# Half of x1 on each expert row: a Mamba and mixture-of-experts kernel without its stored x1 rows

## The reference, cut to what matters

```
x1  = layernorm(x + attn(x))                 # 4096 rows of 256
w, e = softmax(top2(x1 @ gate_w + gate_b))   # two experts a row
ffn = w[0] * expert(e[0], x1) + w[1] * expert(e[1], x1)   # each with its bias b2
out = layernorm(x1 + ffn)
```

## Time and profile before

| | us |
|---|---|
| median of three runs | 1420.89 |
| span of the profiled execution | 1418.7 |
| PE busy | 1272.5 |
| DVE busy | 1090.1 |
| ACT busy | 804.2 |
| POOL busy | 791.7 |

### The profile page before, as it was taken

The page is one execution under the profiler, slowest core; times in us unless marked ns, Lnnn a source line. Parts: engine busy times, 40 slices in busy tenths (PEclk is TensorE's granted clock), DMA queues, the critical chain, the costliest instruction groups (busy, mean ns, idle before and its releaser), DMA issues.

```text
span 1418.7 us, 40444 instructions
## 1 busy us (share of the span) xinstructions
PE 1272.5 (90%) x13336; PEld 1050.7 (74%) x13337; DVE 1090.1 (77%) x2560; ACT 804.2 (57%) x1861; POOL 791.7 (56%) x751
## 2 busy tenths in 40 slices
PE   4889999999999999999888799999999999999970
PEld 2456666666667666666678799999999999999960
DVE  4889999999999999899967877565566656565536
ACT  4667666666666776667545344444454544444436
POOL 3467666767675877788774615234072406152772
PEclk9899999999999999999968999999999999999996
DMA  6213432333443233322235231303012312202594
GB/s 211 81 31 120 135 109 93 96 119 119 135 135 120 84 113 117 123 88 81 87 146 189 72 121 34 121 27 122 30 54 94 105 51 76 72 30 63 134 210 162
DMA packets 90547, 145.73 MB, mean 103 GB/s; under 512 B 9376, under 2 KB 73376, under 8 KB 90336
## 3 DMA queue, kind: packets, MB, share of 16 engines
q1 hardware_dynamic: 75104, 97.03, 21.4%
q0 software_dynamic: 15072, 46.51, 11.2%
q10 hardware_dynamic: 288, 1.19, 0.2%
HBM read 103.03 MB, written 41.67 MB: 102 GB/s over the span
## 4 chain that ended last, share of the span: by engine, by line
PE 48%; DVE 25%; issue 12%; POOL 6%; ACT 5%; DMA 1%; DVEq 1%; SPq 0%; ACTq 0%; POOLq 0%
PE pe L1101 12%; PE pa L1101 12%; PE py L1126 11%; DVE arena L1691 5%; DVE arena L1730 4%; POOL arena L2631 3%; PE pa L676 2%; DVE arena L1738 2%; PE pm L853 2%; PE py L815 2%; DVE arena L1757 2%; DVE arena L1744 1%; PE pt L835 1%; DVE arena L1664 1%; DVE arena L1645 1%
## 5 line engine op out<-in xcount | busy, mean ns | idle before, releaser
L1101 PE MATMUL pe<-arena 128*128 128x128 f16 x3408 | 219.4, 220 | 26.0 <-issue 26.0
L1101 PEld LDWEIGHTS pe<-arena 128*128 128x128 f16 x3408 | 203.4, 98 | 31.3 <-issue 30.6
L1101 PE MATMUL pa<-arena 128*128 128x128 f16 x3408 | 218.8, 220 | 0.0
L1553 ACT ACTIVATE arena<-pe,arena 128x128 f32<-128x128 f32 x568 | 162.0, 371 | 79.8 <-PE pe L1101 78.9
L1101 PEld LDWEIGHTS pa<-arena 128*128 128x128 f16 x3408 | 201.5, 98 | 0.0
L1126 PE MATMUL py<-arena 128*128 (+1 forms) x1704 | 197.7, 273 | 1.3 <-DVE arena L2337 0.9
L1691 DVE SCALAR_TENSOR_TENSOR arena<-pa,arena 128x511 f32<-128x511 f32 (+2 forms) x240 | 178.9, 746 | 11.6 <-ACT arena L1199 5.5
L1126 PEld LDWEIGHTS py<-arena 128*128 128x128 f16 x1704 | 163.4, 98 | 19.6 <-issue 1.8
L2300 DVE SCALAR_TENSOR_TENSOR pm<-pa,arena 128x128 f32<-128x128 f32 x284 | 80.5, 352 | 98.7 <-ACT arena L1553 88.0
L1730 DVE TENSOR_TENSOR_SCAN arena<-arena,pe 128x512 f32<-128x512 f32 x128 | 148.8, 1204 | 3.2 <-issue 1.8
L2531 POOL TENSOR_SCALAR arena<-arena 128x1536 f16<-128x1536 f32 (+2 forms) x35 | 42.6, 1218 | 189.3 <-DVE arena L2337 184.1
(11 more groups left out here) (309 smaller groups left out, 2539.5 us busy)
## 6 DMA issues: line engine op xcount, KB each, us to landing
arena<-step_rows SPq DMA_DIRECT2D x64, 512.0 KB, 6.3
arena<-in_w_exp POOLq DMA_DIRECT2D x32, 768.0 KB, 4.8
arena<-queue SPq DMA_DIRECT2D x74, 129.5 KB, 2.1
answer<-arena SPq DMA_DIRECT2D x71, 128.0 KB, 1.7
arena<-in_x SPq DMA_DIRECT2D x16, 512.0 KB, 6.2
answer<-zeros SPq DMA_DIRECT2D x10, 512.0 KB, 4.8
arena<-h SPq DMA_DIRECT2D x9, 512.0 KB, 5.5
h<-arena SPq DMA_DIRECT2D x8, 512.0 KB, 3.0
```

The lines of the kernel that those rows point to most:

```text
L1101: ins = pe.matmul(bank[:, f * P:(f + 1) * P], w_split[:, p, hl, d * 2 * FF + col:d * 2 * FF + col + P], x[:, r, d, :], start=(n == 0), sto ...
L1553: ins = e.activation(sg[:, half, f, :], GATE[half][:, f * P:(f + 1) * P], ACT.Silu, bias=b1a[:, bass.ds(ex_, 1), ff], scale=1.0 / S1)
```

## The change

The table `x1_rows`, its eight stores and the eight adding transfers are gone. Each token is in two expert rows, and each of the two now gets half of x1: ACT writes `x_half` = 0.5 times the x1 part of `xq` (`rows_halved`, in the place where it made `b_row`, one tile ahead), and DVE makes `b_row` = bias times weight plus `x_half` in a new `rows_added`. SP waits for `x_halved` too before it overwrites `xq`. `x_half` has three buffers of its own. DVE's wait for `x1_back` becomes one for `low_got`.

```
-                if u > NB:
-                    b = u - 1 - NB
-                    sp.wait_ge(x1_ready, b + 1)
-                    sp.dma_start(x1_rows[b * T:(b + 1) * T, :].rearrange("(k p) d -> p k d", p=P),
-                                 x1b[:, 1 - q, :, 0:D]).then_inc(stored[1 - q], 16)
...
             def swap_rows(i, r):
 
                 sp.wait_ge(w_ready, WB * i + (r + 1))
+                sp.wait_ge(x_halved, WB * i + (r + 1))
...
             def epilogue(st):
...
                 h_out(st, 1)
+                rows_halved(0, 0)
                 root_x1(st)
...
+            def rows_halved(i, r):
+
+                at_least(e, b_ready, WB * i + (r - 2))
+                e.activation(x_half[:, r % WB], xq[:, r % WB, 0:D], ACT.Copy, scale=0.5).then_inc(x_halved, 1)
...
                 high_part(i, r, 1)
-                e.wait_ge(w_ready, WB * i + (r + 1))
-                e.sem_inc(hop, 1)
-                e.activation(b_row[:, r], b2a[:, bass.ds(ex_, 1), :].rearrange("p o d -> p (o d)"), ACT.Copy,
-                             scale=w_row[:, r:r + 1]).then_inc(b_ready, 1)
+                rows_halved(i, r + 1)
...
+            def rows_added(i, r, ex_):
+
+                dve.wait_ge(x_halved, WB * i + (r + 1))
+                dve.wait_ge(w_ready, WB * i + (r + 1))
+                if isinstance(i, int) and i == 0 and r == 0:
+                    dve.wait_ge(bias_ready, 2)
+                dve.sem_inc(hop, 1)
+                dve.scalar_tensor_tensor(b_row[:, r], b2a[:, bass.ds(ex_, 1), :].rearrange("p o d -> p (o d)"),
+                                         w_row[:, r:r + 1], x_half[:, r], ALU.mult, ALU.add).then_inc(b_ready, 1)
+
             def second_half(i, r, ex_):
                 gated(i, r, 1, ex_)
+                rows_added(i, r, ex_)
                 low_part(i, r, 1)
...
                 if b == 0:
-                    dve.wait_ge(x1_back, 16 * NB)
+                    dve.wait_ge(low_got, 16 * NTILE)
...
-                if b == 0:
-                    pool.wait_ge(low_got, 16 * NTILE)
-                    for n in range(NB):
-                        pool.dma_start(total[:, n * NK:(n + 1) * NK], x1_rows[n * T:(n + 1) * T, :].rearrange(
-                            "(k p) d -> p k d", p=P), accum_op=ALU.add).then_inc(x1_back, 16)
```

More of the change, by code:

```diff
@@ L169, in build @@
     hx = nc.dram_tensor("hx", [NB, T, D], F32, kind="Internal").ap()
-    x1_rows = nc.dram_tensor("x1_rows", [NTOK, D], F32, kind="Internal").ap()
     queue = nc.dram_tensor("queue", [DUMMY + 4 * P, QW], F32, kind="Internal").ap()
@@ L305, in build @@
         xq = carve(WB, QW)
+        x_half = carve(WB, D)
         b2a = carve(NE, D)
@@ L432, in build @@
         need_ready = sem("need_ready")
-        x1_back = sem("x1_back")
         got = [sem(f"got{b}") for b in range(NB)]
@@ L436, in build @@
         w_half, w_ready, b_ready = sem("w_half"), sem("w_ready"), sem("b_ready")
+        x_halved = sem("x_halved")
         f_scale = sem("f_scale")
@@ L599, in _ @@
                 sp.wait_ge(w_ready, r + 1)
+                sp.wait_ge(x_halved, r + 1)
                 lead_rows(first, WB + r)
@@ L605, in _ @@
             for s in range(2):
-                sp.wait_ge(stored[s], 16 * NB + 16)
+                sp.wait_ge(stored[s], 16 * (NB // 2) + 16)
             with sp.Fori(1, NGRP) as i:
@@ L1257, in chunk_d @@
                 if c.k == 0:
-                    e.wait_ge(stored[c.q], 16 * c.st.h + 16)
+                    e.wait_ge(stored[c.q], 16 * (NB // 2 if c.layer == 1 else c.st.h) + 16)
                 e.wait_ge(out_full, c.n + 1)
@@ L1295, in x1_apply @@
                 before = st.h - 1 if wq == 1 else st.h
-                e.wait_ge(stored[wq], 16 * before + 16)
                 e.wait_ge(scattered[wq], 128 * (before - 4) + 16)
@@ L1583, in _ @@
             high_part(0, 0, 1)
-            e.wait_ge(w_ready, 1)
-            e.activation(b_row[:, 0], b2a[:, bass.ds(first, 1), :].rearrange("p o d -> p (o d)"), ACT.Copy,
-                         scale=w_row[:, 0:1]).then_inc(b_ready, 1)
+            rows_halved(0, 1)
             tile(0, 1, first)
```

## The result

The changed kernel takes 1413.34 us, the median of five runs (1410.45 to 1415.42). The kernel before took 1420.89 us beside it (1419.6 to 1422.71). The ratio is 0.9947, with a 95% interval from 0.9933 to 0.996: faster by 7.5 us, where 8.6 were forecast. The profiled run took 1414.7 us with a span of 1412.7, so 2.0 us lie around the span.

A forecast was written before the change was run, and what follows sets the result against it. PE bounds the expert loop, DVE has slack, and adding transfers crowd out PE's needs behind it. Terms -10.6 + 0.8 + 1.2 = -8.6 us take the median from 1420.89 to 1412.3 us, range 1408.3 to 1417.6.

The forecast's parts named there:

- The adding transfers: Behind the expert loop: without them PE's extra waits and the half clock go, gaining 10.6 us, bounds 4.3 and 12.3.
- 1.0 us that I left in place: PE behind the loop: one ordinary wait of 0.64 us and 0.4 us for new code were expected to stay.
- upper bound of 12.3 us: Tail gain if only the ordinary wait stays and each restart of PE saves its 0.2 us as well.
- the first rival: Behind the loop: the second gathers beside new code suffice for the longest gap; only 4.3 us gained, 1418.6 us; chance 0.11.
- DVE's waits for POOL: In POOL's seven bursts, 21 of the new DVE instructions, both inputs in SBUF, wait 1.0 us each on average.
- the bound of 3.1: The most that one new DVE instruction would wait for POOL in a burst: 3.1 us.
- What the waits cost PE in the loop: In the six bursts of the loop, DVE's late instructions cost 0.8 us, bounds 0 and 7.
- the slack: The queue-row load behind the store of `answer`: lands in 2.1 us, leaving 3.0 us before its `turn`.
- the slower rival: In the bursts DVE falls behind beyond the load's slack; its cost of up to 31 us lands on PE; chance 0.08.
- The early tiles: First burst, tiles 5 and 6: DVE runs late and the `turn` near 831 us waits longer; 1.2 us, bounds 0 and 3.
- ACT, SP and the Mamba stage: ACT's halving replaces an equal copy, and the eight stores and SP's 116.4 us of waiting go without effect: zero.
- The sum: Whole kernel: -10.6 + 0.8 + 1.2 = -8.6 us, span from 1418.7 to 1410.1 us.

The follow-up runs named there:

- experiments 1, 2 and 6: The runs no_adds, both_ways and plain_copy, in that order.
- no_adds: The kernel before without the eight adding transfers, x1 rows still stored, no new DVE instruction: 1410.4 us, ratio 0.9918.
- psum_half: The changed kernel with the new DVE instruction before the first `gated` and the halved x1 in PSUM instead of SBUF: 1410.5 us, ratio 0.9928.
- after_third: The changed kernel run a third time, unchanged: 1413.98 us, ratio 0.9942 against the kernel before.
- both_ways: The changed kernel with `x1_rows`, its eight stores and the eight adding transfers put back, so x1 is added twice: 1422.83 us, ratio 1.0005.
- after_again: The changed kernel run once more, unchanged: 1412.59 us, ratio 0.9943 against the kernel before.
- moved: The changed kernel with `rows_added` moved from between `gated` and `low_part` of half 1 to before the first `gated`: 1411.57 us, ratio 0.9928.
- psum_again: psum_half run once more, unchanged, beside after_third: 1411.09 us, ratio 0.9925 against the kernel before.
- plain_copy: The kernel before with its eight adding transfers made plain copies, overwriting the lower rows: 1413.77 us, ratio 0.9948.
- spread_adds: The kernel before with each adding transfer directly ahead of its own batch's four gathers, DVE still waiting for all eight: 1428.79 us, ratio 1.0052.

## Why the prediction was right

**The adding transfers, forecast 10.6 us, measured 11.5.** The mechanism held as written: no half clock, no wait for queue rows, no wait of PE above 1.02 us before its end, the second gathers directly behind the first. Of the 1.0 us that I left in place 0.5 us stands (0.28 and 0.25 in the profile) and the restarts of PE are saved as well; the result lies midway between the forecast and the upper bound of 12.3 us. That the unnamed waits depend on these transfers, which was a reading of distance in time only, is shown by experiments 1, 2 and 6, and that the longer ones are waits for instructions is what the packets of experiment 1 point to. The bound of 4.3 us, the first rival, is excluded by no_adds, which has every gather and no gap.

**DVE's waits for POOL, forecast 1.0 us on each of 21, measured 26.7 us in all.** It waited in 19, three in each of the six bursts of the loop and one in the first, 1.4 us each; I took the total of L2108 for it and was a quarter short. The longest is 2398 - 476 ns = 1.9 us, under the bound of 3.1. The rule of the Trainium skill ("GPSIMD Engine Reference", the table of the first section), by which VectorE contends for SBUF where both inputs lie there, agrees with psum_half: with one input in PSUM no instance of 71 waited.

**What the waits cost PE in the loop, forecast 0.8 us, measured 1.9.** This term was mis-sized. The step that failed is the slack: "3.0 us", got from a load that lands in 2.1 us, the median of the earlier trace rows. In a burst the loads of the next expert's weights are in flight too. The trace of the kernel before has the packets of the very load that the prediction took, issued at 1058.11: the last ends 3.7 us later, 1.4 us ahead of its `turn`, so the slack was 1.4 us and not 3.0. The loads issued at 895.27 and 972.12 end 1.6 and 1.4 us ahead of theirs. The changed kernel at 894 us:

```profile
894.33 3.10 POOL L2541 TENSOR_TENSOR arena<-arena 128x1536 f16<-128x1536 f32 x1
```

```profile
895.81 1.91 DVE L2321 SCALAR_TENSOR_TENSOR arena<-arena 128x256 f32<-128x256 f32 x1
897.64 0.68 DVE L2304 TENSOR_TENSOR arena<-pz,arena 128x512 f16<-128x512 f32 x1
898.24 0.47 DVE L2345 SCALAR_TENSOR_TENSOR arena<-py,arena 128x256 f32<-128x256 f32 x1
```

```profile
898.96 0.34 SPq L583 DMA_DIRECT2D answer<-arena  x1
900.24 0.35 SPq L577 DMA_DIRECT2D arena<-queue  x1
```

```profile
905.28 0.41 PE L1076 MATMUL pt<-ident,arena 128*128 128x128 f32 x2 [0.45 <-DMA arena<-queue]
906.02 1.19 PE L1098 MATMUL pe<-arena 128*128 128x128 f16 x18 [0.33 <-issue]
```

L2321 waits 1.4 us for POOL's L2541, the result, the store of `answer` and the load behind it go out as late, and the `turn` starts 5.04 us after that load's issue, its packets having ended after 4.5 us, not 2.1. It went out some 1.4 us late and PE waited 0.45, so the load had about 0.9 us of usable slack here. Between the passes at 891.05 and 917.79 us the kernel takes 26.74 us, where it took 25.57 before: 1.2 of the 1.9 us is this one tile. The rest is 0.3 and 0.6 us in the passes that hold the loads issued at 978.21 and 1064.60. Their packets too end only 0.5 us ahead of the `turn`, as at 900.24 (0.6 us), and an unnamed wait of PE follows right behind. The same tile waits in after_third (0.43 us at 904.78) and in both_ways and after_again (0.32 us near 901.3), and in none of `moved`, `psum_half` and `psum_again`. The place, then, turns the wait into time; the slower rival had the right chain, but the price was 1.9 us and not its 31.

**The early tiles, forecast 1.2 us.** From the start of the first group's matmuls to the pass near 836 us it took 28.24 us before and 28.34 after. The `turn` near 831 us waits 0.55 us instead of 0.42, in after_third 1.09, in after_again 2.69. But kernels without the new instruction scatter as much: no_adds waits 0.55 us there and needs 28.29 us for the stretch, plain_copy 1.00 and 28.90, spread_adds 30.45. So neither the sign nor the size of this term is shown; 0.1 us is what the first profile has, 1.2 us what after_third has, and nothing here confirms the term.

**ACT, SP and the Mamba stage, forecast zero.** Nothing of both_ways, which has the stores and SP's waits again, shows a cost of theirs. What the zero left out is that everything ahead of the loop differs by up to 4 us from run to run: the span of the profiled execution is 1418.7 + 3.7 + 1.9 - 11.5 = 1412.8, to rounding.

**The sum, forecast -8.6 us.** Loop and tail together measure -9.7 us in the profiles, where -9.8 was forecast, but that is in part luck: 0.9 us more gain in the tail covers 1.1 us more cost in the loop. The medians of the three sets give -7.5, -9.2 and -7.8 us (the last without the run of 5999.85). The 1.0 us between the median and the forecast is thus less than the start scatters, and no term can be held to account for it. Two small slips in the recorded range change nothing: 12.3 us gained is 1408.6 and not 1408.3, and 6 gained with 3 paid is 1417.9 and not 1417.6.

## What to carry to other kernels

A transfer that nobody waits for can still cost time: ask what else must move while it is in flight, instructions of an engine that enters new code among it, and try first to send it in small pieces, each with a semaphore of its own, before computing its work elsewhere. When such a transfer is spread, look for the one wait that counts all pieces. Take a load's slack from its own packets in the stretch concerned, not from a median. An added VectorE instruction goes to the place with most slack behind it; beside busy GpSimd, one input in PSUM freed it of all waits here, though that alone gained no time over the better place.

## What the runs showed of the hardware

- Adding transfers occupy the DMA engines longer than copies of the same bytes: 202 GB/s at a share of 1.20 against 358 GB/s at 1.03, and 10.61 against 6.07 us for POOL to issue eight of them.
- In the tail, thirteen unnamed waits of PE in eight profiles ended 1.40 to 1.62 us after the end of a 16 KB packet on the instruction queue. With the burst of adding transfers in flight one such packet started 1.8 us after PE had stopped, and PE stood for 4.3 us.
- A load of queue rows took about 1.8 us to its last packet in most tiles of the loop, but 3.0 to 4.5 us in some tiles at and behind the bursts, where loads of expert weights are in flight.
- One and the same program reaches its expert loop up to 4 us earlier or later in different profiles; in one of them the stretch at 1.2 GHz in the first 65 us lay in another place.
- The unnamed waits of PE behind the loop shrank from 7.1 us to between 0.5 and 1.6 without the burst of adding transfers. In all profiles of the changed kernel they were 0.28 and 0.25 us and in `no_adds` 0.48 and 0.90; of these only the 0.90 follows an instruction packet, and what sets the others stays open.
